# Linear attention as a pipeline of chunks, and a residual moved in the scan mixer of a four-layer kernel

## The reference, cut to what matters

```python
def _kernel(x):
    return jax.nn.elu(x) + 1.0
qkv = x @ w_qkv.T                       # q, k, v of 16 heads, 8 channels each
q, k = _kernel(q), _kernel(k)
kv = jnp.einsum('bnhd,bnhm->bhdm', k, v)
z = 1.0 / (jnp.einsum('bnhd,bhd->bnh', q, k.sum(axis=1)) + 1e-06)
out = jnp.einsum('bnhd,bhdm,bnh->bnhm', q, kv, z)
return out.reshape(b, n, d) @ w_out.T + b_out
```

## Time and profile before

| | |
|---|---|
| median of 3 runs | 3545.33 us (3540.59 to 3545.74) |
| the profiled execution's own time | 3559.06 us |
| its span | 3557.4 us, 67038 instructions |
| mean granted TensorE clock | 0.937 |
| PE, weight loads | busy 2974.2 us (84%), 1841.9 us (52%) |
| DVE, ACT, POOL | busy 2358.4 us (66%), 1927.9 us (54%), 1057.7 us (30%) |
| linear attention | first matmul at 873.8 us, last write ends at 1096.2 us |
| scan mixer | first matmul at 1350.4 us, chunks of about 11.16 us |

### The profile page before, as it was taken

How to read it: one execution, slowest core, us unless ns; L and a number is a source line. 1 busy time by engine, 2 the same in 40 slices (tenths; PEclk the granted TensorE clock), 3 DMA queues, 4 the chain that set the end, 5 groups by cost and what they waited for, 6 DMA issues and landing times. The chain is left out here.

```text
span 3557.4 us, 67038 instructions
## 1 busy us (share of the span) xinstructions
PE 2974.2 (84%) x19984; PEld 1841.9 (52%) x19984; DVE 2358.4 (66%) x3518; ACT 1927.9 (54%) x5400; POOL 1057.7 (30%) x1226
## 2 busy tenths in 40 slices
PE   5898778996667977975869999998797999999786
PEld 3576776763443333442636666665334666666332
DVE  4665334665674357964769999996437999999534
ACT  3465344556112264434348888886326888888522
POOL 0233222330000002300035555554105555555400
PEclk9899899998888988987979999999998999999898
DMA  3200111000000000011000000000000000000001
GB/s 120 69 18 21 45 44 29 19 18 4 0 0 7 0 0 14 0 48 27 1 16 1 0 0 0 0 0 1 7 0 16 0 0 0 0 0 0 1 7 47
DMA packets 83880, 51.56 MB, mean 14 GB/s; under 512 B 28752, under 2 KB 76496, under 8 KB 83792
## 3 DMA queue, kind: packets, MB, share of 16 engines
q1 hardware_dynamic: 79696, 42.09, 4.2%
q0 software_dynamic: 4096, 8.40, 0.8%
HBM read 32.11 MB, written 18.35 MB: 14 GB/s over the span
## 5 line engine op out<-in xcount | busy, mean ns | idle before, releaser
L1801 PE MATMUL banks<-wqkv,hf 128*128 128x512 f32 x768 | 438.1, 654 | 78.8 <-ACT qt L1933 48.7
L1920 ACT ACTIVATE probs<-banks,minus_max,rnorm 128x128 f32<-128x128 f32 x1024 | 455.5, 465 | 3.1 <-DVE minus_max L2005 3.1
L1862 POOL TENSOR_TENSOR qk_cross<-qk_raw,rope_scaled 128x512 f32<-128x512 f32 x256 | 351.3, 1392 | 27.2 <-POOL hf L372 15.3
L1847 POOL TENSOR_TENSOR qk_rot<-qk_rot,rnorm 128x512 f32<-128x512 f32 x128 | 184.1, 1438 | 512.5 <-ACT rnorm L1957 505.5
L2035 DVE TENSOR_TENSOR qk_rot<-qk_raw,rope_scaled 128x512 f32<-128x512 f32 x256 | 273.7, 1111 | 22.7 <-ACT qk_raw L1950 22.7
L1985 DVE COPY probs_t<-banks 128x512 f32<-128x512 f32 x256 | 177.1, 692 | 78.9 <-PE banks L1779 75.2
L1920 ACT ACTIVATION_READ_ACCUMULATOR probs<-banks,minus_max,rnorm 128x1 f32 x1024 | 218.2, 213 | 0.0
L735 ACT ACTIVATE probs<-banks,minus_max 128x128 f32<-128x128 f32 (+1 forms) x512 | 208.4, 426 | 16.5 <-DVE minus_max L774 13.4
L2065 PE MATMUL banks<-h_norm,w1t 128*128 x384 | 179.7, 605 | 19.3 <-PEq L213 19.3
L1801 PEld LDWEIGHTS banks<-wqkv,hf 128*128 128x128 f32 x768 | 117.5, 192 | 143.7 <-issue 55.8
L2083 ACT ACTIVATE gelu_g<-banks,b1t 128x512 f32<-128x512 f32 x96 | 66.1, 688 | 219.5 <-PE banks L2065 219.5
(11 more groups left out here) (326 smaller groups left out, 7125.4 us busy)
## 6 DMA issues: line engine op xcount, KB each, us to landing
sorted_x<-zero_rows SPq DMA_DIRECT2D x10, 512.0 KB
rows_in<-sorted_x SPq DMA_DIRECT2D x20, 256.0 KB, 2.8
sorted_y<-rows_out SPq DMA_DIRECT2D x18, 256.0 KB, 2.3
x_res<-in_x SPq DMA_DIRECT2D x8, 512.0 KB
out_x<-x_res SPq DMA_DIRECT2D x16, 256.0 KB, 2.0
w1b<-in_L_ffn_w SPq DMA_DIRECT2D x8, 256.0 KB
s_branch<-in_L_ffn_w SPq DMA_DIRECT2D x8, 256.0 KB
w1g<-in_L_ffn_W SPq DMA_DIRECT2D x8, 256.0 KB, 3.0
```

The source lines that it names most:

```text
L1801: pe.matmul(ps[:, misc(k, j)], hf[:, n // 2 % 2, 0, n % 2 * P:(n % 2 + 1) * P], wqkv[:, w:w + QW], start=True, stop=True).then_inc(*S[name ...
L1847: pool.tensor_tensor(heads, heads, rn[:, (k + 2) % 4, 8:].unsqueeze(2).to_broadcast([P, HEADS, DH]), ALU.mult).then_inc(*S["unit"].inc)
L1862: last = pool.tensor_tensor(by_half(tw[:, n, at]), by_half(qk[:, n, at])[:, :, ::-1, :], tab[:, n, 2 * w + 1].rearrange("p (a d) -> p a d" ...
L1920: last = act.activation(pr[:, k % 2, head], ps[:, 2 * (k % 2) + par, c * P:(c + 1) * P], ACT.Exp, scale=rn[:, k % 4, head:head + 1], bias= ...
```

## The change

In linear attention a chunk is now 512 tokens, two sequences, handled together, and the 16 chunks are written out in a software pipeline of four steps. Round c does: on PE the head sums of chunk c-1, the output projection of c-3, keys, values and queries of c, and the numerators and denominators of c-1; ACT and DVE follow in a matching order. POOL's copy is gone: PE reads xn itself. ACT now reads PSUM: exp and relu of keys and queries (separately, and without the min ahead of exp), the copy of v, the sums of the keys, the scaled mask, and 1e-6 as a bias on the denominators. DVE forms min(exp, 1) + relu from SBUF, masks the product of both sequences at once, and takes one reciprocal and one product of 512 elements. In the scan mixer, `out(c - 1)` moves behind `convolve(c + 1)` on DVE.

The order of each engine in linear attention, from the diff:

```diff
-                with pool.Fori(0, PAIRS) as i:
-                    for u in range(2):
...
-                        pool.tensor_copy(xf[:, u], m["xn"][:, cols(i, u, T)]).then_inc(*S["copied"].inc)
...
             @block.tensor
...
+                for c in range(R + 3):
+                    if 1 <= c < R + 1:
+                        sum_heads(c - 1)
+                    if 3 <= c:
+                        project(c - 3)
+                    if c < R:
+                        key_value(c)
+                        query(c)
+                    if 1 <= c < R + 1:
+                        attend(c - 1)
...
+                def heads(c):
+                    act.wait_ge(*S["heads_ps"].at(0, c))
...
+                    act.activation(ksum[:, c % 2], ps[:, HEADS_AT, 0:2 * (P + 1)].rearrange("p (b d) -> p b d", b=2)[:, :, P],
+                                   ACT.Copy).then_inc(*S["k_sum"].inc)
...
+                    for b in range(2):
+                        last = act.activation(kd[:, c % 2, b], blocks[:], ACT.Copy, scale=ksum[:, c % 2, b:b + 1])
...
+                def features(c):
...
+                    act.activation(ke[:, c % 2].rearrange(pair, n=2), both[:, :, :, 0], ACT.Exp).then_inc(*S["k_exp"].inc)
+                    act.activation(kr[:, c % 2].rearrange(pair, n=2), both[:, :, :, 0], ACT.Relu).then_inc(*S["k_relu"].inc)
...
+                    act.activation(va[:, c % 2, :, 0:P].rearrange(pair, n=2), both[:, :, :, 1], ACT.Copy)\
...
+                    act.activation(qe[:, c % 2], ps[:, Q_AT], ACT.Exp).then_inc(*S["q_exp"].inc)
+                    act.activation(qr[:, c % 2], ps[:, Q_AT], ACT.Relu).then_inc(*S["q_relu"].inc)
...
+                    act.activation(z[:, c % 2], ps[:, DEN_AT], ACT.Identity, bias=tiny[:, 0:1]).then_inc(*S["den"].inc)
+                for c in range(R + 3):
+                    if 1 <= c < R + 1:
+                        heads(c - 1)
+                    if 3 <= c:
+                        out(c - 3)
+                    if c < R:
+                        features(c)
+                    if 1 <= c < R + 1:
+                        denominator(c - 1)
...
+                for c in range(R + 2):
+                    if 1 <= c < R + 1:
+                        n = c - 1
+                        dve.wait_ge(*S["k_sum"].at(0, n))
...
+                        dve.tensor_tensor(kv[:, n % 2],
...
+                    if 2 <= c:
+                        n = c - 2
+                        dve.wait_ge(*S["den"].at(0, n))
+                        dve.reciprocal(z[:, n % 2], z[:, n % 2]).then_inc(*S["z_inv"].inc)
...
+                        dve.tensor_tensor(y[:, n % 2], ps[:, num_bank(n)], z[:, n % 2], ALU.mult).then_inc(*S["weighed"].inc)
+                    if c < R:
...
+                        dve.scalar_tensor_tensor(kp[:, c % 2], ke[:, c % 2], 1.0, kr[:, c % 2], ALU.min, ALU.add)\
...
+                        dve.scalar_tensor_tensor(qp[:, c % 2], qe[:, c % 2], 1.0, qr[:, c % 2], ALU.min, ALU.add)\
```

`sum_heads(c)` waits for k_phi(c) and v(c) and makes four matmuls of 129 columns; `key_value(c)` four of 256; `query(c)` and `project(c)` one of 512 each; `attend(c)` four of 256, the numerators once q_phi(c) and the mask of c are there, the denominators once ACT has scaled the mask. The mask on DVE waits for ACT's k_sum, which reads the same bank ahead of it. Below R is 16. The scan mixer:

```diff
+                    if c + 1 < R:
+                        convolve(c + 1)
                     if c >= 1:
                         out(c - 1)
-                    if c + 1 < R:
-                        convolve(c + 1)
```

More of the change, by code:

```diff
@@ L98 @@
     "value_ps", "high_ps", "padded", "tapped", "convolved", "value", "gate_ps", "gate", "delta_ps", "tanh", "delta", "b_scan", "swept", "both", "fused",
+    "kv_ps", "k_exp", "k_relu", "q_exp", "q_relu", "k_phi", "q_phi", "heads_ps", "k_sum", "k_heads", "kv_heads", "num_ps",
+    "den_ps", "den", "z_inv",
 ]
@@ new lines, in sum_heads @@
+                def sum_heads(c):
+                    pe.wait_ge(*S["k_phi"].at(0, c))
+                    pe.wait_ge(*S["v_sb"].at(0, c))
+                    pe.wait_ge(*S["kv_heads"].at(0, c - 1))
+                    pe.wait_ge(*S["k_sum"].at(0, c - 1))
+                    for b in range(2):
+                        for t in range(2):
+                            mm = pe.matmul(heads_ps(b), kp[:, c % 2, 2 * b + t], va[:, c % 2, 2 * b + t], start=(t == 0),
+                                           stop=(t == 1))
+                    mm.then_inc(*S["heads_ps"].inc)
@@ new lines, in project, with key_value @@
+                def project(c):
+                    pe.wait_ge(*S["weighed"].at(0, c))
+                    pe.wait_ge(*S["o_sb"].at(0, c - 1))
+                    pe.matmul(ps[:, OUT_AT], wout[:], y[:, c % 2], start=True, stop=True).then_inc(*S["o_ps"].inc)
+                def key_value(c):
+                    pe.wait_ge(*S["k_relu"].at(0, c - 1))
+                    pe.wait_ge(*S["v_sb"].at(0, c - 1))
+                    for t in range(4):
+                        mm = pe.matmul(ps[:, KV_AT + t // 2, t % 2 * 2 * P:(t % 2 + 1) * 2 * P],
+                                       m["xn"][:, c * C + t * P:c * C + (t + 1) * P], wq[:, P:3 * P], start=True, stop=True)
+                    mm.then_inc(*S["kv_ps"].inc)
@@ new lines, in query, with attend @@
+                def query(c):
+                    pe.wait_ge(*S["q_relu"].at(0, c - 1))
+                    pe.matmul(ps[:, Q_AT], wq[:, 0:P], m["xn"][:, tokens(c)], start=True, stop=True).then_inc(*S["q_ps"].inc)
+                def attend(c):
+                    pe.wait_ge(*S["q_phi"].at(0, c))
+                    pe.wait_ge(*S["kv_heads"].at(0, c))
+                    pe.wait_ge(*S["weighed"].at(0, c - 2))
+                    for b in range(2):
+                        at = slice(b * T, (b + 1) * T)
+                        mm = pe.matmul(ps[:, num_bank(c), at], kv[:, c % 2, b], qp[:, c % 2, at], start=True, stop=True)
+                    mm.then_inc(*S["num_ps"].inc)
+                    pe.wait_ge(*S["k_heads"].at(0, c))
+                    pe.wait_ge(*S["den"].at(0, c - 1))
+                    for b in range(2):
+                        at = slice(b * T, (b + 1) * T)
+                        mm = pe.matmul(ps[:, DEN_AT, at], kd[:, c % 2, b], qp[:, c % 2, at], start=True, stop=True)
+                    mm.then_inc(*S["den_ps"].inc)
@@ L1166, in _ @@
                 act.preload_act_table_set("exp_and_others")
[L1167 to L1179, removed]
+                act.wait_ge(S["g5"].sem, S["g5"].base + 3)
@@ new lines, in heads @@
+                def heads(c):
+                    act.wait_ge(*S["heads_ps"].at(0, c))
+                    act.wait_ge(*S["k_heads"].at(0, c - 2))
+                    act.activation(ksum[:, c % 2], ps[:, HEADS_AT, 0:2 * (P + 1)].rearrange("p (b d) -> p b d", b=2)[:, :, P],
+                                   ACT.Copy).then_inc(*S["k_sum"].inc)
+                    act.wait_ge(*S["k_sum"].at(0, c))
+                    act.wait_ge(*S["den_ps"].at(0, c - 2))
+                    for b in range(2):
+                        last = act.activation(kd[:, c % 2, b], blocks[:], ACT.Copy, scale=ksum[:, c % 2, b:b + 1])
+                    last.then_inc(*S["k_heads"].inc)
```

121 lines of the change are left out of this document (46 added, 75 removed).

## The result

| | before | after |
|---|---|---|
| median | 3545.02 us (3540.59 to 3545.74, 4 runs) | 3452.80 us (3450.13 to 3454.04, 4 runs) |
| the profiled execution: span, clock | 3557.4 us, 0.937 | 3450.8 us, 0.944 |

The ratio is 0.9741, 95% interval 0.9725 to 0.9758: 92 us less, where 111 were forecast; the forecast of 3434 us was 19 too low, inside the range of 3418 to 3456, 3 us from its upper end.

What follows compares the result with a forecast made beforehand. The chain through all engines, not one engine, was taken as the bound. Linear attention -105 us and scan mixer -6 us made -111, so 3545.33 us became 3434 us; range 3418 to 3456.

Steps and rivals of the forecast that it cites:

- The change is worth what it does to the two stages that it edits: Whole kernel: stages run one after the other, so only linear attention (-105 us) and scan mixer (-6 us) were counted.
- The forecast's own range: Whole kernel: 3420 to 3450 us, from the reciprocal, hand-overs, ends, scan mixer and the shown runs' 5 us.
- the first two rivals: Linear attention: PE's clock falls, or PE's slack is lost in order; chance 0.10 each, range reaching 3418 to 3456 us.
- The ring: Linear attention: k_phi, sum_heads, k_sum, mask, reciprocal, y and hand-overs can't be pipelined and set the period, 6.88 us.
- The ends: Linear attention, fill and drain: k_phi(1) at about 881.6; after k_phi(15), 11.0, then projection 1.9 and last write 0.7.
- PE's clock: Linear attention, rival, chance 0.10: clock 0.88 makes PE need 7.6 us a chunk, 3445 us; at half clock 3511.
- in-order coupling: Linear attention, rival, chance 0.10: PE's slack of 0.2 us is gone, period about 8 us, time 3451 us.
- Table loads: Linear attention, rival, chance 0.02: relu outside exp's table set, 4 loads a chunk on ACT, 3580 us.
- Scan mixer: Taps ahead of the residual save DVE's wait of 0.87 us a chunk, less 0.45 new waiting: -6 us.
- POOL's delta: Scan mixer: it would run only beside the residual, so the scan waits for it, some 0.45 us a chunk.
- the 0.54 that I allowed it: Scan mixer: PE's idle 0.38 us plus 0.15 of drain limits the gain per chunk, bound -7.6 us.
- ACT had written their input before b_scan ended: Scan mixer: the two taps moved first are ready, input written by 1508.37, b_scan's end at 1508.51.

Runs made afterwards that it cites:

- ring_in: The changed kernel with one more 512-element DVE min-and-add per chunk, between y and k_phi in linear attention: ratio to before 0.9759, stage 128.3 us.
- ring_out: The changed kernel with one more 512-element DVE min-and-add per chunk, between k_phi and q_phi in linear attention: ratio to before 0.9751, stage 119.2 us.

## Why the prediction was right where it was, and where it failed

- **"The change is worth what it does to the two stages that it edits": this step failed.** It left out +27.7 us in local attention and the GELU networks. The diff showed the cause: the list of steps of the new stage has q_ps and v_sb in it and no m1. I counted semaphores ("15 semaphores more are primed ... at nothing") and didn't ask what their counts do later. The error of the total is this, with 5 us of the other way from the edited stages.
- **That the range holds the result is in part luck.** The forecast's own range was 3420 to 3450, and 3452.80 lies outside it. The end of 3456 was there for the first two rivals, neither of which came. Nor do the terms give 3450: the lower end is their plain sum (3 + 4 + 1.6 + 5 below 3434), and by the same sum the upper end would be 3458 (2.4 + 3 + 4 + 10 + 5 above). None of these terms is the 27.7.
- **Linear attention: the mechanism was right, the size near.** The ring was forecast at 6.88 and measured at 6.46, and ring_in and ring_out show that it is the ring. The mis-sized term is the head sums with their hand-over, 1.38 + 0.13 forecast, 1.20 measured. The row of 1.38 is not at a low clock (1.00 granted in 963.57 to 964.95): it merges the four matmuls of u=0 and the four of u=1, and before the second four PE waits for k_phi of u=1, which DVE ends at 964.17. Eight without that wait take 1.16. The 0.13 was read behind a projection at a granted clock of 0.50; here it is 0.04. k_sum with its hand-over is 0.20 for 0.30; y, with its 0.61, and the reciprocal, 3.34 for 3.35, were as forecast. 14 periods of 0.42 less make 5.9 us; the stage gave 109.7 for the 105 forecast. The ends were right: k_phi(1) came 9.9 us after ACT's table load (10.0 forecast), and the last write 13.4 after k_phi(15) starts (13.6).
- **PE's clock and in-order coupling** (the first two rivals) didn't come: clock 1.00 and PE 6.34 busy of 6.46. **Table loads**: one in the stage; Relu runs beside Exp at 0.59 us without a load. The Trainium skill (ScalarE: Activation LUTs, Rules for kernel authors) wants relu on VectorE; ring_in prices what that would cost here, 0.60 us a chunk for every instruction that DVE gets inside the ring, while ACT is busy 4.77 of 6.46.
- **Scan mixer: a total near the forecast by a wrong path, which is luck.** -6.3 for -6 (-5.1 and -5.2 in two other profiles). The scan doesn't wait for POOL's delta. PE's 0.38 of idle time per chunk has gone, and with PE busy 10.80 of 10.80 nothing more is to be had from DVE's order. That is 0.36 a chunk: what bounds the gain is PE, by less than the 0.54 that I allowed it, and not POOL's delta. DVE's waiting has moved: the timeline shows it in front of the first tap, behind ACT, and in a longer second tap.

```profile
1340.56 1.28 DVE L1523 SCALAR_TENSOR_TENSOR b_scan<-delta_tanh,val 128x512 f32<-128x512 f32 x2
1342.13 0.75 DVE L1513 SCALAR_TENSOR_TENSOR conv<-v_pad,cw,conv 128x512 f32<-128x512 f32 x1 [0.28 <-ACT conv L1443]
1342.91 0.98 DVE L1516 SCALAR_TENSOR_TENSOR conv<-v_pad,cw,conv 128x512 f32<-128x512 f32 x1
1343.82 0.74 DVE L1507 SCALAR_TENSOR_TENSOR s_branch<-banks,bout,xn 128x512 f32<-128x512 f32 x1
1344.48 1.21 DVE L1534 TENSOR_TENSOR_SCAN scans<-delta,b_scan 128x514 f32<-128x514 f32 x1
```

  "ACT had written their input before b_scan ended" held for the old timing alone; with DVE no longer held up by PE it comes 0.28 too early. POOL's two deltas (4.43 together, where they took 4.36) run from 1338.93 to 1343.36 and so end before the residual starts: the first ends at 1342.33, just behind DVE's wait of 0.28, the second within the second tap. That POOL has the port while the second tap is drawn out from 0.75 to 0.98 is argued from the timeline, not tested.

## What to carry to other kernels

Write down the ring with its hand-overs and read every engine's slack from it: an instruction inside cost its full length every period here, one outside nothing, as long as it fitted into the idle time. Where waits compare with values that a loop computes, a semaphore that is used again carries its history with it: give a rewritten stage names of its own, let the steps of one loop enter it with equal counts, and compare the compiled loops of the stages that weren't edited. And compare all stages, not only the edited ones; a race for a shared port can turn 0.16 us into 0.67 us a round.

## What was not expected of the hardware

A register instruction of 0.03 us, by carrying a wait that the weight load had carried before, made PE start 0.16 us late, and by the lost race for the port this became 0.67 us a round, 20 to 22 us in the two stages. A semaphore increment added 0.14 us on PE: 116 of them, 15.8 us (207.1 less 191.3); 140 of them in the kernel before, 18.1 us (215.7 less 197.6). The reciprocal stays linear, 3.34 us for 512 elements after 1.75 for 256. ACT's column sums, 2 elements a partition read from PSUM, took 0.17 us, below the 0.245 that was the nearest row.
